# Subtracting the row mean from each decoded block of weights on VectorE in place of ScalarE

## The reference

```
attn = einsum('ds,td->st', w1, w2) * sparse_mask      # 1024 x 1024, a narrow band
y    = gelu(x @ attn + b2)                            # exact gelu
x    = layernorm(x + y)
w_l  = lut4[o, 4-bit code of (o, i)]                  # 1024 x 1024, a table of 16 values per row o
y    = x @ w_l.T + bias                               # 8-bit table instead where |x| > 64
x    = layernorm(x + y)
```

## Time and profile before

| | us |
|---|---|
| median of 3 runs (lowest, highest) | 309.78 (309.44, 309.96) |
| the profiled execution: its own time | 310.19 |
| the profiled execution: span, first to last instruction | 308.4 |
| PE busy in the span | 292.0 (95%) |
| PEld busy | 255.9 (83%) |
| DVE busy | 196.3 (64%) |
| ACT busy | 184.1 (60%) |
| POOL busy | 109.6 (36%) |
| chain that ended last: PE, DVE, ACT, DMA | 79%, 9%, 3%, 2% |

### The profile page before, as it was taken

The page is one execution under the profiler, slowest core; times in us unless marked ns, Lnnn a source line. Parts: engine busy times, 40 slices in busy tenths (PEclk is TensorE's granted clock), DMA queues, the critical chain, the costliest instruction groups (busy, mean ns, idle before and its releaser), DMA issues.

```text
span 308.4 us, 5056 instructions
## 1 busy us (share of the span) xinstructions
PE 292.0 (95%) x1907; PEld 255.9 (83%) x1907; DVE 196.3 (64%) x349; ACT 184.1 (60%) x244; POOL 109.6 (36%) x179
## 2 busy tenths in 40 slices
PE   7899889999999999999999999999999999999960
PEld 3788666776668999999999999999998888888860
DVE  2669898986858979798876786504134535342461
ACT  1866659787988968877896979251145443213110
POOL 4000003342443989898788200000033333333220
PEclk9999999999999999999999999999999999999996
DMA  7999999999989410110101111119147785342322
GB/s 231 397 355 356 337 348 278 245 264 219 199 146 203 100 35 34 36 36 34 36 34 37 51 48 40 53 38 299 40 143 257 252 285 200 143 170 104 123 115 80
DMA packets 28320, 49.36 MB, mean 160 GB/s; under 512 B 2432, under 2 KB 11904, under 8 KB 28288
## 3 DMA queue, kind: packets, MB, share of 16 engines
q1 hardware_dynamic: 23376, 40.36, 38.5%
q0 software_dynamic: 4352, 8.39, 15.4%
q10 hardware_dynamic: 560, 0.20, 0.2%
HBM read 36.36 MB, written 12.58 MB: 159 GB/s over the span
## 4 chain that ended last, share of the span: by engine, by line
PE 79%; DVE 9%; ACT 3%; DMA 2%; issue 2%; SPq 1%; POOL 1%; POOLq 0%; DVEq 0%; ACTq 0%
PE acc L547 19%; PE acc L549 19%; PE acc L548 19%; PE acc L530 5%; PE acc L476 5%; PE acc L420 3%; DMA w<-in_w2d 2%; PE acc L453 2%; PE acc L486 2%; PE acc L455 2%; PE acc L454 2%; PE acc L463 2%; DVE zz L1014 1%; DVE dest L972 1%; ACT z L694 1%
## 5 line engine op out<-in xcount | busy, mean ns | idle before, releaser
L547 PE MATMUL acc<-lin,zz 128*128 128x256 f32 (+2 forms) x424 | 130.2, 307 | 0.3 <-issue 0.3
L549 PE MATMUL acc<-lin,zz 128*128 128x256 f32 (+2 forms) x424 | 129.8, 306 | 0.0
L548 PE MATMUL acc<-lin,zz 128*128 128x256 f32 (+2 forms) x424 | 129.6, 306 | 0.0
L547 PEld LDWEIGHTS acc<-lin,zz 128*128 128x128 f32 x424 | 80.0, 189 | 4.6 <-issue 0.5
L548 PEld LDWEIGHTS acc<-lin,zz 128*128 128x128 f32 x424 | 80.2, 189 | 4.0
L549 PEld LDWEIGHTS acc<-lin,zz 128*128 128x128 f32 x424 | 80.1, 189 | 4.1
L712 ACT ACTIVATE leaf<-planes,lut,flip 128x1024 f32<-128x1024 uint8 x56 | 67.5, 1238 | 0.6 <-DVE dest L972 0.6
L972 DVE COPY_PREDICATED leaf<-planes,leaf 128x1024 f32<-128x1024 uint8 x32 | 43.6, 1361 | 12.4 <-ACT leaf L712 11.6
L1354 POOL DMA_DIRECT2D z<-in_xr x16 | 19.6, 1225 | 73.7 <-ACT z L694 73.7
L814 ACT ACTIVATE junk<-rows,cols 128x1024 bf16<-128x1024 f32 x15 | 17.3, 1152 | 41.7 <-POOL cols L1328 41.6
L1326 POOL TENSOR_TENSOR cols<-cols 128x1 f32<-128x1 f32 x15 | 9.5, 634 | 78.0 <-DVE rows L1089 78.0
(11 more groups left out here) (105 smaller groups left out, 437.7 us busy)
## 6 DMA issues: line engine op xcount, KB each, us to landing
z<-in_xt SPq DMA_DIRECT2D x16, 512.0 KB, 9.8
z<-in_xr POOLq DMA_DIRECT2D x16, 512.0 KB, 8.3
out_rows<-rows SPq DMA_DIRECT2D x15, 512.0 KB, 2.9
out_rows<-parts SPq DMA_DIRECT2D x32, 128.0 KB, 1.9
rows<-out_rows SPq DMA_DIRECT2D x16, 256.0 KB, 2.8
w<-in_w1d SPq DMA_DIRECT2D x7, 512.0 KB, 9.0
off_band<-in_mask_rest SPq DMA_DIRECT2D x8, 448.0 KB, 4.1
w<-in_w2d SPq DMA_DIRECT2D x3, 584.0 KB, 9.3
```

Source lines behind the costliest of these rows:

```text
L547: nc.tensor.matmul(bank, hi, w_hi, start=k == 0, stop=False)
L548: nc.tensor.matmul(bank, hi, w_lo, start=False, stop=False)
L549: last = nc.tensor.matmul(bank, lo, w_hi, start=False, stop=k == KB - 1)
```

## The change

The function `centre` leaves the scalar block and comes back in the vector block as a `tensor_scalar` with one per-row operand. On DVE it stands in step 5, behind `mean_of_row` and behind merge 1 of the next block. The general path is not touched.

```
-            def centre(b):
-                act.wait_ge(row_mean_made, b + 1)
-                nc.scalar.activation(dest[:, b % 2, :], dest[:, b % 2, :], ACT.Identity,
-                                     bias=neg_row_mean[:, b:b + 1]).then_inc(centred, 1)
...
-                if b == KB and i not in (3, 5):
+                if b == KB and i != 3:
                     pass
                 elif i == 3 and b:
                     sum_rows(b - 1)
-                elif i == 5 and b:
-                    centre(b - 1)
...
+            def centre(b):
+                dve.wait_ge(row_mean_made, b + 1)
+                nc.vector.tensor_scalar(dest[:, b % 2, :], dest[:, b % 2, :], neg_row_mean[:, b:b + 1], None,
+                                        ALU.add).then_inc(centred, 1)
...
                     if b < KB:
                         merge(b, (2, 5, 6, 8, 10).index(i))
+                    if i == 5 and b:
+                        centre(b - 1)
```

## The result

| | us |
|---|---|
| before, median of 7 runs (lowest, highest) | 309.78 (309.10, 310.17) |
| changed, median of 7 runs (lowest, highest) | 311.56 (309.99, 312.21) |
| ratio changed to before, 95% interval | 1.0046 (1.0025 to 1.0068) |
| profiled execution of the changed kernel: its own time, span | 312.21, 310.4 |

The change makes the kernel slower, by 1.4 us by the ratio and 1.8 by the medians, and the runs of the changed kernel scatter over 2.2 us where those of before scatter over 1.1. The predicted time was 310.5, its range 309.6 to 311.2: the direction was right, the size too small, and the median lies outside the range.

A forecast was written before the change was run, and what follows sets the result against it. The prediction took PE to be the bound, with DVE's queue the path at the end of the front. A 0.75 us slide less 0 gain, on the 309.78 median, gave 310.5 us, range 309.6 to 311.2.

The forecast's parts named there:

- Nor does TensorE's clock change: End of the front: PE's clock stays at 2.4 GHz although its gap grows from 1.52 to 2.27 us.
- DVE's queue bounds the end of the front: From about 21 to 36.27 us DVE's queue is the path; whatever is put into it there moves the end.
- Gain of ACT's freed time, 0: Eight ACT instructions of 1.15 us removed, in front, group 2 and linear stage: nothing gained, since PE waits for none.
- paced by ACT: Rival: ACT sets the pace in the mixing stage, so freeing it closes waits: -0.59 us, 309.2 us; chance 0.09.
- Slide of block 0, 0.75: Front, ahead of the mask strip at 31.97: the new DVE instruction delays all behind it, x_lo included, by 0.75 us.
- Carried on in full: Behind 36.4 us the 0.75 us delay reaches the end whole; no later PE wait takes it up.
- Group 2 and the linear stage, 0: Blocks 1 to 7: DVE's pauses and waits hide the new instructions, 0 us; the tightest hand-over has 1.03 us.
- PE's first L453 at 37.1 to 37.3, after a wait of 2.2 to 2.4: Sign of a right forecast: PE's first mixing matmul starts then in place of 36.41, having waited for x_lo.
- The mix_e wait as before, near 42.9: Sign of a right forecast: PE's 0.63 us wait for DVE's mix_e, at 42.15 before, stays but slides.

The follow-up runs named there:

- the repeat: The changed kernel run again unaltered, 12 executions beside the kernel before: median 310.63 us, ratio 1.0027.
- The step moved out of it: Kernel before, with one decoder step (a leaf on ACT, a merge on DVE) moved from the front into mixing group 0: 309.00 us, ratio 0.9974.
- Blocks 1 to 7 alone: Changed kernel with block 0's centring left on ACT and only blocks 1 to 7 centred on DVE: 309.85 us, ratio 1.0004.
- all eight with block 0 later: Changed kernel with block 0's centring and identity moved behind the last x_lo of group 0 on DVE: 309.91 us, ratio 1.0004.
- the gap filled: Changed kernel with constant-data matmuls on PE between its last strip and its wait for x_lo: eight 310.51 us, three 310.24 us.
- the second pass: Changed kernel with block 0 passed twice on DVE (adding 0.0): 311.34 us; with twelve constant matmuls in PE's gap: 310.81 us.

## Why the prediction was wrong

The step that failed is the sentence on the clock: "Nor does TensorE's clock change". It rested on the row of 35.00 to 36.40 us, in which PE ran nothing and the clock was granted at 1.00. That row shows that a wait of 1.52 us does no harm. It shows nothing of one of 2.05 or 2.27, and the prediction said itself that such a gap "would have to end differently". It then gave this case neither a price nor a chance. The profile had no stretch at half clock in the mixing stage to take a price from, so the range should have reached further up. What came in place of the full clock: 0.50 for 6.77 us in the profiled execution, at 1.58 us net, and by the mean clock such a fall in 9 of 19 executions of the changed kernel.

That the number fell outside the range was in part the draw: four of the seven executions had fallen, so the median is that of a fallen one. The median of the twelve of the repeat, 310.63, and that of all 19, 310.75, lie inside the range. The missing step would have been missing all the same.

- **DVE's queue bounds the end of the front**: right. The step moved out of it, its place there and the slide all act as said.
- **Gain of ACT's freed time, 0**: right. Blocks 1 to 7 alone change nothing, nor do all eight with block 0 later. ACT's idle time before its mix_hi grew from 2.36 us to 2.80, as forecast. Of the rival "paced by ACT" nothing is seen: the 0.62 us wait of DVE's x_lo for x_hi is 0.66 now.
- **Slide of block 0, 0.75**: somewhat too big. The instruction takes 0.75 (0.743 to 0.770 in eight), between the cast and the row with two operands, and the next starts 0.78 behind. But it also starts 1.20 us behind the merge's start, where the mask strip had to wait 1.36: the sum is 1.20 + 0.78 - 1.36 = 0.62. I had asked how the new instruction overlaps with its neighbours, and not which old wait it takes over.
- **Carried on in full**: right where the clock stays up. With the gap filled, the change costs +0.6 to +0.8 us, and with the second pass +1.2 to +1.4. No later wait takes it up. The forecast of 310.5 is the time of this part: 310.51 and 310.24 were measured with the gap filled.
- **Clock**: wrong, see above. In the profiled execution 1.58 us; between the medians of fallen and other executions 311.80 - 310.08 = 1.7.
- **Group 2 and the linear stage, 0**: right, by the rows above and by blocks 1 to 7 alone.
- **PE's first L453 at 37.1 to 37.3, after a wait of 2.2 to 2.4**: it came at 37.58, in part through the late load, and after 2.05, where a slide of 0.62 makes 2.14.
- **The mix_e wait as before, near 42.9**: wrong in the profiled executions that fell, where PE comes later than mix_e; right with the gap filled (42.97, 0.63). Calling it "the next start that PE waits for" was a misreading: the wait of 0.53 us at 39.89 comes before it. With the clock up this one slides too (40.72 after 0.54 us with eight matmuls in the gap), so the sum was not touched.

The sum of the parts, 0.62 + 9/19 x 1.7 = 1.4 us, can be held against the mean of the 19 executions, 310.85, less that of the 37 of before beside them, 309.65: 1.2 us. The agreement is rough: the ten that did not fall lie between 308.4 and 311.7 and on average only 0.3 above before, less than the slide. The +1.8 of the first comparison is more than a typical launch loses.

The Trainium skill (TensorE: Matmul & The Clock Gate, "Part 1: The HAM clock gate (the "warmup" mystery)") has the gate at full or at half rate depending on recent PE activity, and says that the point of transition differs from run to run of one kernel. The runs agree on both: the clock read 1.00 before the fall and 0.50 in it, matmuls put into the gap kept it from falling, and the same program falls in some executions and in others not. By that rule a longer wait of PE was a risk of this change, and it stood in no case of the prediction.

## What to carry to other kernels

An instruction put into a queue that leads PE costs its own slide, and, if PE waits longer for it than it has waited before anywhere in the trace, possibly a stretch at half clock worth more than the slide. A row that shows full clock in a short gap is no evidence for a longer one. When runs of a kernel split into groups, compare their mean granted clocks before looking for contention, and test it by giving PE matmuls on constant data in the gap.

## What the runs showed of the hardware that was not expected

- With PE idle for 1.5 us between two busy stretches no execution fell by the measure of 0.982 (93 of the kernel before, 12 with three matmuls in the gap, 24 with blocks 1 to 7 alone or block 0 later); a fall of 3.4 us would hardly show in a mean clock, and none stands in the profiled executions of these. With 2.05 to 2.14 us, 12 of 30 fell, and two more, at 0.985 and 0.986, may have had a short fall. What lies between was not tried.
- The clock can fall after PE has gone back to work (PE at 37.58, the fall at 38.56), so the slow matmuls do not stand right behind the gap that precedes them.
- The half-clock stretch was 6.8 us long in the two profiles of the changed kernel, and 3.4 in that of the double pass, whose gap was longer. What sets its length and which executions fall stays open.
